# Attention maxima in two 64-row tiles side by side, both pairs of a step next to each other in TensorE's queue, half chunks packed two to a bank

## The reference, cut to what matters

```python
q = jnp.einsum('bsd,de->bse', x, Wq) + bq      # x: 16 x 3136 x 32, layer-normed tokens
k = jnp.einsum('bsd,de->bse', x, Wk) + bk
v = jnp.einsum('bsd,de->bse', x, Wv) + bv
scores = jnp.einsum('bqd,bkd->bqk', q, k) / jnp.sqrt(d)
attn = jax.nn.softmax(scores, axis=-1)
out = jnp.einsum('bqk,bkd->bqd', attn, v)
```

## Time and profile before

| | |
|---|---|
| time, median of 3 runs | 3278.15 us (3275.57 to 3279.92) |
| profiled execution: span, first to last instruction | 3274.6 us |
| the span against the median of the runs | 3.6 us less |
| mean granted TensorE clock | 0.874 of full speed |
| attention: first maxima matmul to last copy's start | 768.55 to 2739.34 us |
| TensorE / VectorE / ScalarE busy | 83% / 73% / 51% |

### The profile page before, as it was taken

One profiled execution on the slowest core, in us unless ns is written; L12 is line 12 of the kernel. 1 busy time (PEld: TensorE's weight loads), 2 busy tenths in 40 slices (PEclk: granted clock), 3 DMA queues, 4 the chain that ended last, 5 costly groups with the idle time before them and its releaser, 6 DMA issues. The chain is left out here.

```text
span 3274.6 us, 59408 instructions
## 1 busy us (share of the span) xinstructions
PE 2707.3 (83%) x18550; PEld 1134.9 (35%) x18550; DVE 2388.6 (73%) x4220; ACT 1673.0 (51%) x2250; POOL 273.3 (8%) x260
## 2 busy tenths in 40 slices
PE   2756465657999999999999999999999995777776
PEld 0322232321233333333333333333333322666665
DVE  4355554557888888888888888888888810788887
ACT  0242333341166666666666666666666684333332
POOL 0000000000000000000000000000000000354555
PEclk9978687875599999999999999999999997666667
DMA  5583857523001101101100110110110002222220
GB/s 127 122 206 124 201 147 177 151 100 124 0 0 45 45 0 45 44 0 44 45 13 32 44 45 0 44 44 0 45 45 0 20 20 80 74 90 69 79 89 20
DMA packets 49873, 213.04 MB, mean 65 GB/s; under 512 B 9446, under 2 KB 22370, under 8 KB 41058
## 3 DMA queue, kind: packets, MB, share of 16 engines
q1 hardware_dynamic: 48298, 207.71, 21.4%
q10 hardware_dynamic: 1464, 3.95, 0.3%
HBM read 75.25 MB, written 74.60 MB: 46 GB/s over the span
## 5 line engine op out<-in xcount | busy, mean ns | idle before, releaser
L1027 DVE TENSOR_REDUCE at_XM<-at_psX 128x448 f32 x2425 | 1369.5, 617 | 224.9 <-PE at_psX L893 212.2
L991 ACT ACTIVATE at_PR<-at_psS 128x896 f32<-128x896 f32 x1344 | 1159.8, 915 | 535.1 <-PE at_psS L880 534.2
L893 PE MATMUL at_psX<-at_KS,at_US 128*128 (+1 forms) x2800 | 945.0, 370 | 52.3 <-DVE at_XM L1027 33.1
L880 PE MATMUL at_psS<-at_US,at_KS 128*128 (+1 forms) x2800 | 769.9, 355 | 22.9 <-DVE at_mrow L1041 15.2
L908 PE MATMUL at_psV<-at_PR,at_V 128*32 128x448 f32 x5376 | 648.4, 554 | 2.4 <-ACT at_PR L991 2.4
L893 PEld LDWEIGHTS at_psX<-at_KS,at_US 128*128 128x128 f16 x2800 | 231.2, 98 | 711.8 <-DVE at_XM L1027 435.3
L880 PEld LDWEIGHTS at_psS<-at_US,at_KS 128*128 128x128 f16 x2800 | 250.6, 98 | 364.9 <-issue 111.1
L1050 DVE TENSOR_REDUCE at_XM<-at_psX 128x1 f32<-128x448 f32 x375 | 212.4, 618 | 53.2 <-PE at_psX L893 51.1
L1338 POOL TENSOR_TENSOR fi_WE<-fi_WE 128x256 f32<-128x256 f32 (+1 forms) x224 | 213.0, 979 | 172.8 <-DVE fi_WE L1392 172.0
L1344 POOL TENSOR_TENSOR fi_T<-fi_T,fi_RES 128x800 f32<-128x800 f32 x16 | 30.0, 1872 | 2112.3 <-DVE fi_T L1407 2112.3
L326 PE MATMUL psA<-sb_stacks,sb_lhs 128*32 128x448 f32 x1568 | 170.3, 563 | 23.5 <-DMA sb_stacks<-sb_T 10.5
(11 more groups left out here) (179 smaller groups left out, 2001.6 us busy)
## 6 DMA issues: line engine op xcount, KB each, us to landing
sb_stacks<-sb_Xp SPq DMA_DIRECT2D x64, 496.8 KB, 11.8
sb_stacks<-sb_T SPq DMA_DIRECT2D x64, 443.0 KB, 8.1
sums<-at_O SPq DMA_DIRECT2D x16, 1568.0 KB, 6.1
fi_SUMS<-sums SPq DMA_DIRECT2D x16, 1568.0 KB, 6.7
at_KS<-key_stacks SPq DMA_DIRECT2D x16, 784.0 KB, 7.4
at_US<-query_stacks SPq DMA_DIRECT2D x16, 784.0 KB, 8.9
key_stacks<-sb_KS SPq DMA_DIRECT2D x13, 784.0 KB, 4.6
query_stacks<-sb_YU SPq DMA_DIRECT2D x13, 784.0 KB, 3.6
```

What stands on the lines that cost most here:

```text
L880: last = nc.tensor.matmul(psS[:, u % 2, j, 0:TILE], KS[:, b, c * P:(c + 1) * P], US[:, b, bass.ts(t, TILE)], start=True, stop=True)
L893: nc.tensor.matmul(psX[:, bank, 0:TILE], US[:, b, c * P:(c + 1) * P], KS[:, b, bass.ts(t, TILE)], start=True, stop=True).then_inc(x_full, 1)
L991: nc.scalar.activation(PR[:, u % 4], psS[:, u % 2, :, 0:TILE], ACT.Exp).then_inc(p_ready, 1)
L1027: nc.vector.tensor_reduce(XM[:, bass.ds(t, 1), c:c + 1], psX[:, bank, 0:TILE].unsqueeze(1), AX.X, ALU.max).then_inc(x_done, 1)
```

## The change

The maxima are made from 64 rows of the stacks instead of 128. A second copy of the upper 64 rows of the queries is loaded into `UH`, partitions 64 to 127. `maxima(m, pair)` issues two matmuls, one on array rows 0 to 63 (`US`, `KS`), one on rows 64 to 127 (`UH`, `KS`), into two neighbouring banks of the ring of three. It waits once, for `x_done >= at - 1`: every place of the ring but the last one before the pair must have been reduced. For a step's second pair that is the first of the two reduces of the step's first pair. VectorE still reduces one bank at a time.

The half chunk leaves the tiles: at an image's start, four banks hold the half chunk of all seven tiles, two tiles to a bank (64 partitions each), both for maxima (`pair < 2`) and for scores (`i < 2`, two `Exp` of 896 columns). An image is now 43 steps (`STEPS`): two `scores` (four matmuls), then `maxima` twice (four reduces), then `sums` of one quad. Maxima run six steps further ahead (`AHEAD = 6`). `PR` has six slots instead of four. The turn no longer makes TensorE wait for `mrow_ready`; scores of an image wait for `m_in`. All loops are written out: no registers, no branches. There are six loads per image instead of three, and four row DMAs instead of two.

```diff
-        PR = sb("PR", [P, 4, 2, TILE])
+        AHEAD = 6
+        PR = sb("PR", [P, PRS, 2, TILE])
...
+        def pairs_of(n, s):
+            m, first = (n + 1, 2 * (s + AHEAD)) if s + AHEAD < STEPS else (n + 2, 2 * (s + AHEAD - STEPS))
+            return [(m, first), (m, first + 1)] if m < N else []
...
-            def maxima(n, b, t, c):
-                base = (n * NT + t) * NC + FREE_X
-                bank = 1 if c == NC - 1 else c % 3
-                if c == NC - 1:
-                    pe.wait_ge(x_done, base + c - 1)
-                elif c == 1:
-                    pe.wait_ge(x_done, base)
-                else:
-                    pe.wait_ge(x_done, base + c - 2 - (c == 0))
-                nc.tensor.matmul(psX[:, bank, 0:TILE], US[:, b, c * P:(c + 1) * P], KS[:, b, bass.ts(t, TILE)],
-                                 start=True, stop=True).then_inc(x_full, 1)
+            def maxima(m, pair):
+                b, at = m % B, place(m, pair)
+                if pair == 0:
+                    pe.wait_ge(k_in[b], 16 * LOADS * (m // B + 1))
+                if at + 1 >= 3:
+                    pe.wait_ge(x_done, at - 1)
+                for j in range(2):
+                    u = (US, UH)[j][HALF * j:HALF * j + HALF, b]
+                    k = KS[HALF * j:HALF * j + HALF, b]
+                    o = psX[:, (at + j) % 3, 0:TILE]
+                    if pair < 2:
+                        for h, t in enumerate(half_tiles(2 * pair + j)):
+                            last = nc.tensor.matmul(o[HALF * h:HALF * h + HALF], u[:, TF:T], k[:, t * TILE:(t + 1) * TILE],
+                                                    start=True, stop=True)
+                    else:
+                        t, c = divmod(pair - 2, NF // 2)
+                        c = 2 * c + j
+                        last = nc.tensor.matmul(o, u[:, c * P:(c + 1) * P], k[:, t * TILE:(t + 1) * TILE],
+                                                start=True, stop=True)
+                    last.then_inc(x_full, 1)
...
+            for n in range(N):
+                for s in range(STEPS):
+                    for i in (2 * s + 2, 2 * s + 3):
+                        if i < SU:
+                            scores(n, i)
+                        elif n + 1 < N:
+                            scores(n + 1, i - SU)
+                    ahead(n, s)
+                    behind(n, s)
+                    if s >= 1:
+                        sums(n, s - 1)
```

More of the change, by code:

```diff
@@ L819, in attend, with first_place, place, turn_place @@
         block = ctx.enter_context(nc.Block())
[L820 to L827, removed]
+        def first_place(m):
+            return 0 if m == 0 else 2 * XPAIRS + (m - 1) * (2 * XPAIRS + 1)
+        def place(m, pair):
+            return first_place(m) + 2 * pair + (m >= 1 and pair >= 1)
+        def turn_place(m):
+            return first_place(m + 1) + (2 if m + 1 < N else 0)
@@ L829, in _, with half_tiles, turns @@
+        def half_tiles(bank):
+            return 2 * bank, min(2 * bank + 1, NT - 1)
+        def pairs_of(n, s):
+            m, first = (n + 1, 2 * (s + AHEAD)) if s + AHEAD < STEPS else (n + 2, 2 * (s + AHEAD - STEPS))
+            return [(m, first), (m, first + 1)] if m < N else []
+        def turns(n, s):
+            return s + AHEAD == STEPS and n + 1 < N
         @block.sync
         def _(sp):
[L831 to L834, removed]
@@ L837, in max_rows @@
+            def max_rows(n):
                 sp.wait_ge(mrow_ready, n + 1)
                 for h in range(2):
[L839 to L845, removed]
@@ L847, in _ @@
-            sp.dma_start(ident[:], scr["ident"]).then_inc(c_in, 16)
-            sp.wait_ge(zeroed, 1)
-            for b in range(B):
[L850 to L867, removed]
+                    row = US[C * (2 * h + 1):C * (2 * h + 1) + 1, n % B]
+                    sp.dma_start(row[:, 0:TF].rearrange("a (k c) -> a k c", k=NF), mrow[1:NC, h]).then_inc(m_in, 16)
+                    sp.dma_start(row[:, TF:T], mrow[0:1, h, 0:HALF]).then_inc(m_in, 16)
+            def store(n):
+                sp.wait_ge(o_ready, n * NT + NT)
+                sp.dma_start(scr["sums"][n], O[:, n % B]).then_inc(o_out[n % B], 16)
@@ L869, in _ @@
+            sp.dma_start(ident[:], scr["ident"]).then_inc(c_in, 16)
+            for n in range(B):
+                load(n)
+            max_rows(0)
+            for n in range(N):
+                if n + 1 < N:
+                    max_rows(n + 1)
+                store(n)
+                if n + B < N:
+                    sp.wait_ge(v_full, (n + 1) * NT)
+                    load(n + B)
+            for b in range(B):
+                sp.wait_ge(o_out[b], 16 * len(range(b, N, B)))
         @block.tensor
@@ L870, in _ @@
         def _(pe):
[L871 to L881, removed]
-                last.then_inc(s_full, 1)
@@ L896, in turn_max, with scores @@
[L896 to L906, removed]
+            def scores(n, i):
+                b, at = n % B, n * SU + i
+                if i == 0:
+                    pe.wait_ge(m_in, 64 * (n + 1))
+                if at >= 2:
+                    pe.wait_ge(p_ready, at - 1)
+                for j in range(2):
+                    if i < 2:
+                        for h, t in enumerate(half_tiles(2 * i + j)):
+                            last = nc.tensor.matmul(psS[HALF * h:HALF * h + HALF, i, j, 0:TILE], KS[:, b, TF:T],
+                                                    US[:, b, t * TILE:(t + 1) * TILE], start=True, stop=True)
+                    else:
+                        t, c = divmod(i - 2, NF // 2)
+                        c = 2 * c + j
+                        last = nc.tensor.matmul(psS[:, i % 2, j, 0:TILE], KS[:, b, c * P:(c + 1) * P],
+                                                US[:, b, t * TILE:(t + 1) * TILE], start=True, stop=True)
+                last.then_inc(s_full, 1)
@@ new lines, in turn_max, with sums @@
+            def turn_max(m):
+                at = turn_place(m)
+                pe.wait_ge(x_done, at - 2)
+                pe.wait_ge(negm_ready, 2 * m + 2)
+                nc.tensor.transpose(psX[0:NC, at % 3, 0:P], negm[:], ident[:]).then_inc(x_full, 1)
+            def sums(n, q4):
+                b, (t, k) = n % B, divmod(q4, QUADS)
+                pe.wait_ge(p_ready, n * SU + 2 * q4 + 4)
+                if k == 0 and n * NT + t >= 1:
+                    pe.wait_ge(o_ready, n * NT + t)
@@ L907, in sums @@
                 for q in range(G):
                     last = nc.tensor.matmul(psV[C * q:C * q + C, 0:TILE], V[:, b, G * k + q, :],
-                                            PR[:, (2 * k + q // 2) % 4, q % 2, :], start=(k == 0), stop=(k == NQ - 1))
+                                            PR[:, (2 * q4 + q // 2) % PRS, q % 2, :], start=(k == 0), stop=(k == QUADS - 1))
                 last.then_inc(p_used, 1)
[L912 to L959, removed]
@@ L961, in _ @@
-            pe.wait_ge(c_in, 16)
[L962 to L978, removed]
@@ L979, in _ @@
-            for n in range(FULL * B, N):
-                step(n, n % B, N - 1 - n)
+                if k == QUADS - 1:
+                    a, w = HALF * (t % 2), TILE // G
+                    for q in range(G):
+                        last = nc.tensor.matmul(psV[C * q:C * q + C, q * w:(q + 1) * w], V[a:a + HALF, b, NF, :],
+                                                PL[a:a + HALF, n % 2, t // 2, q * w:(q + 1) * w], start=False, stop=True,
+                                                skip_group_check=True)
+                    last.then_inc(v_full, 1)
@@ new lines, in ahead, with behind @@
+            def ahead(n, s):
+                pairs = pairs_of(n, s)
+                if pairs:
+                    maxima(*pairs[0])
+                if turns(n, s):
+                    turn_max(n + 1)
+            def behind(n, s):
+                pairs = pairs_of(n, s)
+                if pairs:
+                    maxima(*pairs[1])
+            pe.wait_ge(c_in, 16)
+            for pair in range(XPAIRS):
+                maxima(0, pair)
+            for s in range(STEPS - AHEAD, STEPS):
+                ahead(-1, s)
+                behind(-1, s)
@@ L982, in _ @@
+            scores(0, 0)
+            scores(0, 1)
+            for n in range(N):
+                for s in range(STEPS):
[8 more added lines that the diff above has]
+                        sums(n, s - 1)
         @block.scalar
@@ L995, in tile_body @@
-            def tile_body(n, b, t, more=True):
-                j = n * NT + t
-                base = j * NU
-                for u in range(2, NU):
-                    exponentials(base, j, u)
-                if more:
-                    for u in range(2):
-                        exponentials(base + NU, j + 1, u)
-                act.wait_ge(v_full, j + 1)
-                nc.scalar.activation(O[:, b, bass.ts(t, TILE)], psV[:, 0:TILE], ACT.Copy).then_inc(o_ready, 1)
-            act.wait_ge(zeroed, 1)
```

(66 more changed lines are left out.)

107 lines of the change are left out of this document (53 added, 54 removed).

## The result

The changed kernel takes 3561.46 us (median of 3 runs, 3560.38 to 3561.95) against 3278.15: 1.0865 times the time before, 95% interval 1.0847 to 1.0882. The span of its profiled execution is 3559.7 us.

What follows compares the result with a forecast made beforehand. TensorE's own work was taken as the bound, VectorE 15% behind. Scores' start at 902, images 2008 and end 100 put the last copy near 3010, +271 us on 3274.6; forecast 3550 us, range 3440 to 3675.

Steps and rivals of the forecast that it cites:

- The step: Four chunks in the middle of a tile: 1.07 + 0.29 + 0.89 + 0.76 + 0.10 = 3.11 us, before 2.51.
- The shape change: Before a step's first pair, the array's change to 64-row tiles costs 0.10 us; without it 64 us fall away.
- pairs in series: Rival: a pair's two 64-row matmuls don't run side by side; +121 us, giving 3671; chance 0.10.
- The clock: Rival: the granted clock falls to 0.50 in the steps, 4.9 us each, giving about 4700 us; chance 0.04.
- The image: One image of 43 steps, with half chunk and turn: 135.1 us, 17.2 more than before the change.
- the half chunk's sums: Seven times per image, right behind other sums: 0.25 us each, 1.8 together.
- the turn: Once per image, the second pair waits for both reduces of the first: 0.53 us more.
- VectorE's pattern: In each step, reduces in twos with about 0.3 and 0.7 us between, VectorE idle a third of the time.
- Start and end: Maxima alone at the low clock, scores beginning at 898; 49 last steps without maxima, 2.04 each, 100 us.
- The hidden wait: Rival: the wait between the two pairs is covered; step 2.23 us, -562 us, giving 2988; chance 0.05.

Runs made afterwards that it cites:

- e1: The changed kernel with the sums of a quad moved between a step's two pairs of maxima matmuls: 3085.33 us, 0.9407 of the kernel before.
- e2: The changed kernel with its order kept, but each matmul of a pair waits for its own bank only: 3542.38 us.
- e3: The changed kernel, but each maxima reduce reads 224 of its bank's 448 columns: 3386.1 us.
- e7: The changed kernel with the sums between the pairs and each maxima reduce reading 224 of 448 columns: 3043.04 us.
- e4: The changed kernel, but each maxima matmul uses all 128 rows, order and waits kept: 3617.92 us.

## Why the prediction was right

- **The step.** Forecast 3.11 us, measured 3.13: 1.08 for 1.07, 0.29, 0.89, and 0.86 for 0.76 + 0.10. That TensorE's queue holds everything behind the waiting pair was the deciding reading, and e1, e2, e3 and e7 show it from four sides. This was no luck.
- **The shape change.** Taken at the upper bound, 0.10 us, from another kind of change: 0.86 against e4's 0.77 confirms its size. The rule that the prediction cites (the Trainium skill, "TensorEngine Tiling (Array Packing)", section "Key Properties": changing the tiling mode drains TensorE) agrees with these 0.09 us. That the drain is their cause is not shown: in the changed kernel the weight load of a first pair also starts together with its matmul (1504.26), where in e4 it starts 0.19 us ahead (1503.68 against 1503.87), and no run tells the two apart.
- **Side by side.** The rival of pairs in series is refuted by starts 0.01 us apart.
- **The clock.** It was 0.50 in the stretch of maxima alone, as assumed, and 1.00 from 909 us to 3024 us, turns included. The low clock that I allowed for at each turn did not come: at the turn shown above TensorE idled 1.10 us. The rival is refuted.
- **The image.** Forecast 135.1 us, measured 136.6. Mis-sized was the half chunk's sums: 0.33 us (3.45 less 3.13 for the step that has them), not 0.25, so 0.6 per image; the step's 0.016 gives 0.7; the turn 0.62, not 0.53.
- **VectorE's pattern was read wrong.** The prediction has its reduces in twos, with about 0.3 us idle between the pairs. By its own prices the third reduce has its bank 1.47 us after the first pair (1.07 + 0.36 + 0.04), and at one reduce every 0.53 us VectorE comes to it at 1.46 (0.36 + 0.04 + 2 x 0.53). The trace has all four in 2.23 us without a gap. The step doesn't hang on it, but the rival in e2's expectation does.
- **Start and end.** Scores began at 895.4, forecast 898. The end without maxima took 93 us, from the last turn's transpose (2929.7) to the last copy's start (3022.8), where I had 100: 49 steps at 1.9 us, close to the exponentials' own pace of 3.85 for two quads, not 2.04. These two partly cancel the images' 21 us, and what is left is 11.5 us of 283. That it is so little is in part luck.
- **The hidden wait.** The rival put its price at 562 us, for a step of 2.23 with three changes of shape. Nothing passed the waiting pair, as the prediction held; hiding the wait took another order of the queue. With the sums in between there are four changes of shape and the step is 2.34, and the order was worth 476 us.

## What to carry to other kernels

A wait in an in-order queue costs what stands behind it, so ask of each wait which instruction releases it and what lies between that one's cause and the wait in the same queue. Two users of a small ring of buffers that stand next to each other put a round trip through the other engine between them (here 1.07 us); independent work of at least that length between them makes it free, and places where that work is missing (here step 0 and the turn) keep the wait. Only then does making the waiting instructions faster pay in full: the same tiles were in a kernel 8.7% slower and in one 6.6% faster.

## What was not expected of the hardware

- With the pairs far enough apart, weight loads still "wait" in the views (in e1, 1013 times between 910 and 2300 us, 546.9 us in total, as this row of its waits shows) while TensorE's matmuls wait 23 us in the same stretch:

```profile
PEld at_psX L925 <- DVE at_XM L1027: 546.9, 1013, 1.0
```

- Attention's first matmul, which waits for the first load, started between 769.6 us (e3) and 776.1 us (e1) in kernels that issue the same loads: up to 6 us that are in any comparison of single profiles here.
